# Cross-attention and a routed feed-forward on one core: the chunks of sequences regrouped, and POOL's transfers each tied to a step of PE

## What is computed

```python
x = x + tanh(g_xattn) * attention(layernorm(x), ctx, ctx, wq, wk, wv)   # 16 heads of depth 8
x = x + tanh(g_ffn) * ffn(layernorm(x))
# ffn: for each row, 2 of 8 experts by router logits, gates = softmax over the two
h = relu(x @ W1[e] + b1[e])          # 128 -> 256
out = sum over e of gate[e] * (h @ W2[e] + b2[e])
```

## Time and profile before

| | |
|---|---|
| three runs | 770.36, 763.18, 769.44 us; median 769.44 us |
| the profiled execution | 766.2 us, its span 764.5 us |
| granted PE clock, mean | 0.882 of 2.4 GHz |
| busy share of the span | PE 78%, PE weight loads 56%, DVE 49%, ACT 48%, POOL 35% |
| indirect transfers of POOL | 112 scatters (mean 974 ns) and 112 gathers (mean 958 ns) |

### The profile page before, as it was taken

The page is one execution under the profiler, slowest core; times in us unless marked ns, Lnnn a source line. Parts: engine busy times, 40 slices in busy tenths (PEclk is TensorE's granted clock), DMA queues, the critical chain, the costliest instruction groups (busy, mean ns, idle before and its releaser), DMA issues.

```text
span 764.5 us, 18488 instructions
## 1 busy us (share of the span) xinstructions
PE 598.7 (78%) x6213; PEld 428.8 (56%) x6213; DVE 373.2 (49%) x1361; ACT 368.2 (48%) x835; POOL 263.9 (35%) x281
## 2 busy tenths in 40 slices
PE   2559997878888797859889868998877679789467
PEld 0235554544556574546666646676546568678346
DVE  2447778847556436645554555544434132112134
ACT  5127665644446554436556445655544445334112
POOL 5020110153000336530434344434563662641720
PEclk9969999986789999879899779999878979989769
DMA  4445654444444525374637265662422425452211
GB/s 109 117 105 149 158 134 118 100 144 128 101 114 57 129 71 145 63 128 74 150 82 147 78 123 75 111 128 73 91 64 71 122 88 138 105 104 76 66 38 42
DMA packets 158121, 78.65 MB, mean 103 GB/s; under 512 B 85088, under 2 KB 153312, under 8 KB 158032
## 3 DMA queue, kind: packets, MB, share of 16 engines
q1 hardware_dynamic: 119760, 45.65, 28.0%
q10 hardware_dynamic: 31104, 17.13, 8.3%
q0 software_dynamic: 7168, 14.69, 7.7%
HBM read 30.72 MB, written 36.75 MB: 88 GB/s over the span
## 4 chain that ended last, share of the span: by engine, by line
PE 56%; issue 10%; DVE 8%; DMA 8%; ACT 6%; another core or an unknown queue 6%; SPq 4%; ACTq 2%; DVEq 0%
PE y L607 9%; PE scores L503 8%; PE bank_oT L517 7%; PE max_scores L482 5%; DMA xsT<-xs_dram 4%; PE o L530 3%; PE hidden_p L593 3%; PE hidden_p L591 3%; ACT hidden L807 2%; PE hidden_p L592 2%; DVE neg_max L1025 2%; PE o L647 2%; PE bank_oT L647 2%; PE group L458 2%
## 5 line engine op out<-in xcount | busy, mean ns | idle before, releaser
L1025 DVE TENSOR_REDUCE neg_max<-max_scores 128x4 f32<-128x308 f32 x244 | 116.3, 477 | 191.8 <-PE max_scores L482 178.8
L741 ACT ACTIVATE probs<-scores 77x512 f32<-77x512 f32 x256 | 150.0, 595 | 86.8 <-PE scores L503 74.9
L1351 POOL DMA_INDIRECT back<-ys_dram,at x112 | 107.3, 958 | 118.5 <-PE scores L503 53.7
L1336 POOL DMA_INDIRECT xs_dram<-rows,at x112 | 109.1, 974 | 108.5 <-PE scores L503 79.1
L517 PE MATMUL bank_oT<-probs,v_cols 77*9 77x128 f32 x2048 | 111.0, 292 | 10.8 <-ACT probs L741 5.2
L503 PE MATMUL scores<-q_st,k_st 128*77 128x128 bf16 x1024 | 114.8, 241 | 1.9 <-issue 1.7
L482 PE MATMUL max_scores<-k_st,q_st 128*128 128x308 bf16 x244 | 79.6, 326 | 40.3 <-DVE neg_max L1025 20.6
L503 PEld LDWEIGHTS scores<-q_st,k_st 128*77 128x77 bf16 x1024 | 79.0, 127 | 53.6 <-issue 45.4
L807 ACT ACTIVATE hidden<-hidden_p,b_cols 128x128 f32<-128x128 f32 x260 | 74.2, 370 | 68.9 <-PE hidden_p L593 63.6
L607 PE MATMUL y<-w_sb,hidden 128*128 x608 | 102.9, 317 | 0.0
L607 PEld LDWEIGHTS y<-w_sb,hidden 128*128 128x128 f32 x608 | 92.4, 218 | 3.5 <-issue 0.2
(11 more groups left out here) (144 smaller groups left out, 939.2 us busy)
## 6 DMA issues: line engine op xcount, KB each, us to landing
ys_dram<-ys ACTq DMA_DIRECT2D x38, 256.0 KB
q_st<-q_dram SPq DMA_DIRECT2D x16, 512.0 KB, 5.1
k_st<-k_dram SPq DMA_DIRECT2D x64, 77.0 KB
xs_all<-x SPq DMA_DIRECT2D x16, 256.0 KB, 3.9
q_dram<-q_hl SPq DMA_DIRECT2D x16, 256.0 KB
xs_dram<-zeros_b ACTq DMA_DIRECT2D x16, 256.0 KB, 3.4
out<-xs_all SPq DMA_DIRECT2D x16, 256.0 KB
k_dram<-k_hl SPq DMA_DIRECT2D x48, 77.0 KB
```

What stands on the lines that cost most here:

```text
L741: nc.scalar.activation(probs[h][:], score_bank[h % 2][0:KEYS, :], ACT.Exp, scale=SCALE).then_inc(s_exp, 1)
L1025: V.tensor_reduce(neg_max[:, i // 2, :, h, i % 2], max_to(b, h)[:, 0:PER * KEYS].rearrange("p (j k) -> p j k", j=PER), AXIS_X, ALU.max, ne ...
L1336: G.indirect_dma_start(out=xs_dram[c % 2], out_offset=bass.IndirectOffsetOnAxis(ap=at[k][c % 4][:, i:i + 1], axis=0), in_=rows[c % 2][:, i ...
L1351: G.indirect_dma_start(out=back[k][:, b % 16, :], out_offset=None, in_=ys_dram[c % 2][0:TILES[c] * 128, :], in_offset=bass.IndirectOffsetO ...
```

## The change

The chunks become 12, 12, 12, 12 and 8 sequences. Behind the attention the plan places two sequences a slot instead of three, and each transfer of POOL waits for a step of PE of its own. Since the order of the chunks asks for it, `gate` gets a fifth buffer (and with it every index modulo 4 of `gate` becomes modulo 5). The core of the diff:

```diff
-CHUNKS = (8, 12, 12, 12, 12)
+CHUNKS = (12, 12, 12, 12, 8)
...
-        for _ in range(3 if late else 2):
+        for _ in range(2):
...
-        gate = [[sb(f"gate{k}_{i}", [128, NMAX]) for i in range(4)] for k in range(2)]
+        gate = [[sb(f"gate{k}_{i}", [128, NMAX]) for i in range(5)] for k in range(2)]
...
-                if c >= 4:
-                    dve.wait_ge(s_sum, SEQ0[c - 3])
+                if c >= 5:
+                    dve.wait_ge(s_sum, SEQ0[c - 4])
...
                 if t < LAST_ATT:
                     pool.wait_ge(p_st, clip(HG * (t - SCORE_LAG) + 2 * n + k, HG * B))
-                elif k == 0:
+                    return
+                if quads_at(t):
                     if n == 0:
-                        pool.wait_ge(p_hid, 2 * quads_before(t))
-                    if n == 1:
-                        pool.wait_ge(p_hid, 2 * quads_before(t) + len(quads_at(t)))
-                    if n >= 2:
+                        pool.wait_ge(p_hid, 2 * quads_before(t) + k)
+                    elif k == 0:
                         pool.wait_ge(p_y, quads_before(t))
-                    if dense_before(t):
-                        pool.wait_ge(p_dhid, HC * dense_before(t))
+                    else:
+                        pool.wait_ge(p_hid, 2 * quads_before(t) + 2)
+                if dense_at(t):
+                    if n == 0:
+                        pool.wait_ge(p_dhid, HC * dense_before(t) + k)
+                    elif k == 0:
+                        pool.wait_ge(p_dhid, HC * dense_before(t) + HC)
+                    elif dense_at(t - 1):
+                        pool.wait_ge(p_dy, dense_before(t))
```

More of the change, by code:

```diff
@@ L1104, in make_gates @@
                 n, r = SIZES[c], ROUTE * c + (BOTH if c < NC else CHOSEN)
-                first, second = gate[0][c % 4][:, 0:n], gate[1][c % 4][:, 0:n]
+                first, second = gate[0][c % 5][:, 0:n], gate[1][c % 5][:, 0:n]
                 dve.wait_ge(s_gexp, c + 1)
@@ L1117, in gates_of_all @@
             def gates_of_all():
-                first, second = (gate[k][NC % 4][:, 0:DENSE].unsqueeze(2).to_broadcast([128, DENSE, E]) for k in range(2))
+                first, second = (gate[k][NC % 5][:, 0:DENSE].unsqueeze(2).to_broadcast([128, DENSE, E]) for k in range(2))
                 dve.wait_ge(s_rt, ROUTE * NC + CHOSEN + 4)
@@ L1201, in add_experts @@
                 dve.wait_ge(s_rt, ROUTE * c + GATED)
-                V.scalar_tensor_tensor(out=to, in0=back[0][:, b % 16, :], scalar=gate[0][c % 4][:, i:i + 1], in1=to,
+                V.scalar_tensor_tensor(out=to, in0=back[0][:, b % 16, :], scalar=gate[0][c % 5][:, i:i + 1], in1=to,
                                        op0=ALU.mult, op1=ALU.add).then_inc(s_half, 1)
                 dve.wait_ge(s_half, b + 1)
-                V.scalar_tensor_tensor(out=to, in0=back[1][:, b % 16, :], scalar=gate[1][c % 4][:, i:i + 1], in1=to,
+                V.scalar_tensor_tensor(out=to, in0=back[1][:, b % 16, :], scalar=gate[1][c % 5][:, i:i + 1], in1=to,
                                        op0=ALU.mult, op1=ALU.add).then_inc(s_sum, 1)
```

## The result

The changed kernel takes **726.05 us** (median of 724.68 to 734.05, 4 runs) where the kernel before takes 769.90 beside it: ratio **0.948, 95% interval 0.938 to 0.958**. The forecast was 741.9 us, a gain of 27.5; the gain is 40 in the spans of the two profiled executions (764.5 and 724.0) and 44 in the medians.

What follows compares the result with a forecast made beforehand. No engine fills the span; chains between engines bound it, with PE's signals late during POOL's transfer runs. Terms +0.5 - 6 - 12.5 + 2.5 - 12 = -27.5 us give 741.9 us from 769.4, range 721 to 765.

Steps and rivals of the forecast that it cites:

- the second rival: Pacing clears nearly all: late slots pay 0.4 us each, the end of dense units 2 us; 718.9 us, chance 13%.
- dense end: Last 24 gathers, slots 92 to 97: a stuck PE soon runs POOL dry; 11 us lost, not 22.9, gain 12.
- one quad less: Attention slots: a quad moved out to the late slots saves 3.5 us there.
- slot 77's burst: Slot 77: five unheld gathers in a row vanish; gain 6 us, or 3.7 if only PE's idle time goes.
- one quad more: Late slots: the quad moved out of the attention costs 4.0 us there.
- Paced transfers in late slots: Slots 78 to 91: four transfers each, held to own steps, cost 1.4 us a slot, 19.6 for 32.1; gain 12.5.
- ACT's store of quad 32: Slot 88: the store waits for late gathers and delays the ReLU behind it; costs 2.5 us, between 0 and 6.
- runs of POOL hold nobody: Rival, late slots and dense units: late signals have another cause; +3 us, 772.4 us, no change; chance 12%.
- The slower case: Rival, 14 late slots: spread transfers disturb each by 3.6 us; 785 us, slower from 2.5 us a slot; chance 8%.
- the announced signs: Profile after: no run above four transfers to slot 91, unnamed waits a third, late quad slots 7 us or less.
- The clock behind the attention: Sign in the profile after: granted clock above 0.9 behind the attention.
- the theory: Behind the attention: while POOL works off transfers back to back, PE's signals arrive a microsecond or two after the run.

Runs made afterwards that it cites:

- `hold_77`: The kernel before, with each gather of slot 77 waiting for its own step of that slot's quad; 768.48 us, ratio 1.000 (0.995 to 1.004).
- `thin_79_80`: The changed kernel with one sequence (two transfers) each in slots 79 and 80 and everything behind a slot later; 737.09 us, too spread for a ratio.
- `no_wait_at_end`: The kernel before, with its last 24 gathers waiting for no step of PE, only for the stores; 768.93 us, ratio 1.002 (0.997 to 1.007).
- `end_spread`: The changed kernel with one sequence back, not two, in slots 93, 95, 97 and 99; 717.84 us, ratio 0.937 (0.931 to 0.943) against the kernel before.

## Why the prediction held, and what in it was off

The mechanism of the forecast was right and the time lies in its range, but near the low end: 726.05 is nearer to the second rival's 718.9 than to 741.9. The late slots and the dense end kept less of their loss than I had priced, and a gain ahead of copy 76 had no term; all three errors point the same way. The terms against the two traces, along the same places of the program:

| place | forecast | measured |
|---|---|---|
| up to the end of PE's work in slot 77: one quad less | -3.5 | -3.5 |
| the same, all else (forecast: slot 77's burst) | -6 | -8.8 |
| late slots: one quad more | +4.0 | +4.0 |
| the same, all else (transfers -12.5, the store +2.5) | -10 | -16.7 |
| dense end | -12 | -15.5 |
| **sum** | **-27.5** | **-40.5** |

The quads are taken at the forecast's prices in both columns; the rest is what the traces leave. The first mark cuts a quad in the kernel before: the output product of slot 77's quad falls behind it, into slot 78. So up to the mark the difference is only two halves, and the late slots of the changed kernel have 14 pairs of halves but 13 output products. An output product is 2.2 us of PE's work at the full clock (four times 0.56, from 573.64 on), and by so much the -8.8 could be -11 and the -16.7 be -14.5. The sum stays.

*Slot 77 and the attention.* The mark stands at 580.0 and not 592.3, 12.3 us less. From copy 76 on it is 18.9 against 8.3 us. Counted as two quads less that leaves 10.6 - 7.0 = 3.6 us for the burst, the smaller of my two values; but slot 76's first half lies ahead of the copy (from 572.59), so it is three halves (0.7 us each) and one output product less, and by PE's work 10.6 - 4.3 = 6.3 us are left, the 6 that I took. The trace doesn't decide between the two. Ahead of copy 76 it is 1.7 us less with one quad more (23 outputs copied in place of 22), or one quad without that first half, so 4.5 to 5.2 us for which I had no term. It is no accident of one trace: copy 76 stands at 568.6 to 571.7 in the six traces with the new order of chunks and at 573.4 to 580.3 in the eight with the old one, averages 570.0 and 576.5. As many transfers, 142, lie ahead of it in both. Which slots became cheaper I did not try to find. `hold_77` shows besides that the term was argued too locally: taking the burst away by waits brings nothing while the slots behind are full; it counts here because the transfers are gone from slot 77 and the slots behind have room.

*Paced transfers in late slots.* The largest error of the forecast by the table, and about as large as the one ahead of slot 78 if the output product is counted where it runs. I gave each of 14 slots 1.4 us, 19.6 in all, between 5.6 and 29.4. Measured the same way, 14 quads of 4.0, some 5.5 units of 3.52 and 1.6 for the transposes make 77.0 of 90.9 us, so 13.9 are excess (16.1 with 13 output products). They are not spread evenly: 21.7 - 13.6 = 8.1 (or 10.3) in slots 78 to 80, and 69.2 - 63.4 = 5.8 in the eleven slots from 81 to 91, 0.5 a slot. Not all of the first is POOL's. PE stands idle there for 5.75 us: 2.79 of it (up to 593.86) follow the late copy at 591.97 behind the six transfers, but 1.43 and 1.53 are waits for a ReLU that had started on time. By the code the halves of quads up to slot 79 share one bank and from slot 80 on they have two, so in slots 78 and 79 PE must wait for ACT's ReLU of each half before it starts the next. The clock of 0.70 comes on top. That is the lower end that I had from slots beside a quad (0.4), and not the middle that I chose because POOL's 5 us fill more of a late slot. In these eleven slots POOL is busy for 41.30 of 69.20 us, so how full POOL is did not set the price. That it is the interleaving with PE's steps is my reading; no run varies it alone.

*ACT's store of quad 32.* +2.5 expected. The wait is there and longer than said, 5.54 us and not 2 to 3, but slot 88 takes 7.4 us between the ends of PE's second halves, as slots 84 and 86 do (7.3, 7.5): nothing is to be seen of it. By the code PE's second half doesn't need the ReLU of the first, which would be why. The caution was right one slot on, where `thin_79_80` pays 4.3 us for it. The gather's landing, which no row of before had, is at most 2.70 us from the start of its issue to the store (652.46 to 655.16), 1.75 without the 0.95 of the issue, and so under the 3.9 that I took as its upper end. The 2.6 that the prediction gives beside this term can't be worked out again from its own parts: the middle of 0 to 2.5, 0.95 and 2.0, less 2, is 2.2.

*The dense end.* Units 6 to 14 lose 7.6 us (35.8 - 28.2) where I had 11 and before 22.9, which is 15.3 of the 15.5. The picture was the one given: POOL falls behind, a stuck PE runs it dry, and the signals come through in the pause. The longest standstill of PE is 2.56 us, as foretold under 5.

*The rivals.* That runs of POOL hold nobody is refuted, and by an experiment and not by coincidence: the loss of 22.9 us goes to nothing in three kernels that only take the indirect transfers away. The Trainium skill (Trainium Architecture — The Big Picture, section What this means for kernel authors) says that the engines are independent and hold each other only through semaphores. The traces differ from it: in `no_wait_at_end`, where DVE's addition waits for nothing of POOL's, it came 23 us after PE's product, and PE's own matmuls came one each 2.1 us. The slower case asked for 2.5 us a slot, and the 14 slots paid 1.0 to 1.15 on average. The second rival, nearly all cleared, had the price of slots 81 to 91 right (0.4 against 0.5), but not slots 78 to 80 and not the end, where 7.6 us are lost and not 2. Of the announced signs two were wrong: there is a run of six transfers up to slot 91, and late slots with a quad are 6.5 us on average but not each at 7 or less (slots 79 and 80 take 18.1 together, slot 84 7.3, slot 86 7.5). The clock behind the attention holds as a mean only: it is 0.70 in slots 78 to 80, where PE is busy for 15.95 of 21.70 us, and 1.00 and 0.97 behind. ACT's unnamed waits fell to 10.3 us, a little over the third.

*Where the theory was too wide and too narrow.* It said "while POOL works off transfers". In the two kernels that tried it, plain transfers on POOL and computing on it hold nobody. The forecast didn't suffer, since all of POOL's transfers here are indirect. And it said that signals come late, where PE's own issuing is slowed too.

## What to carry to other kernels

A run of indirect transfers on POOL is not work beside the others: in these kernels it holds back the other engines, so keep each one behind a step of PE, with a pause after every few. Spreading worked only where the neighbouring slots had room; taken from one slot and pushed into full ones, a burst cost the same. And before everything is shifted by a slot, look for the wait that has exactly one slot of slack.

## What the runs showed of the hardware that was not expected

- A run of 24 indirect transfers of 0.95 us, one each 1.255 us, makes eight dense units take 50.7 us and not 28.2. DVE takes up a finished product of PE 23 us late, 4 us after the run. After runs of six and eight, ACT and DVE start 1.5 to 1.8 us after the run's end, which is 2.1 and 5.7 us after PE was done (ACT at 591.97, DVE at 690.12 in the changed kernel). In the last 5 us of the long run PE issues matmuls that wait for nothing at one each 2.1 us, then 1.4, and at full rate 4 us after its end.
- 24 plain transfers of the same size on the same queue of POOL take 0.53 us each and cost 0.0 us; 24 power operations of 0.99 us each in a row cost 0.0 us. The Trainium skill (DMA: Bandwidth & Descriptors, section SWDGE vs HWDGE vs iDMA) puts plain and indirect transfers of GpSimd on the same software path, and the trace agrees (7168 packets on the software queue with either kind); for who is held, the two are not alike. Why isn't shown, nor whether it is the lookup itself or the scattered rows: the trace has no row for what stands between the engines' queues and their semaphores.
- Programs that are identical up to a place reach it at times up to 5 us apart by the end of the late slots (670.6 and 665.5 us in the changed kernel and `end_spread`), and up to 7 by copy 76 (573.4 and 580.3 in the kernel before and `no_wait_at_end`), so one trace of each is not enough to price an edit of 2 us.
